# Where the shifted copies of the offset maps come from: nine copies within SBUF, or one write to memory and three shifted reads

## The chip, the cores and the metric

The kernel runs on one core of one Trainium2 chip. The metric is the device time of one execution in microseconds (us).

## The reference, cut to what matters

Input `x` is (4, 128, 32, 32) in float32: four images of 128 channels and 32 x 32 pixels. Two residual layers follow each other.

```python
x = x + L0(_gn(x), W, b)            # group norm, then a mixing of all pixels by squared cosine scores
x = x + L1(_gn(x), w1, b1, w2, b2, wd)

def L1(x, w1, b1, w2, b2, wd):
    offset = conv2d_same(conv2d_same(x, w1, b1), w2, b2)    # 3x3 convolutions, 128 and then 72 channels
    return relu(deform_conv(x, offset, wd, k=3, pad=1, dg=4))

def deform_conv(x, offset, wd, k=3, pad=1, dg=4):
    off = offset.reshape(B, dg, K, 2, H, W)                 # 4 groups x 9 taps x (dy, dx) = 72 maps
    ...
    val = gather(y0, x0) * (wy0 * wx0)[:, :, None] + ...    # bilinear sample at each tap's place
    return jnp.einsum('ogck,bgckhw->bohw', wr, val)
```

The 72 offset maps say, for each pixel, where each of the nine taps of each of the four groups samples the image.

## The kernel before

The four images (batches b = 0 to 3) are worked on one after the other, with the engines' programs written out by hand as loops over slots: a batch has 72 slots n = 9 t + k, for eight tiles t of four image rows. While batch b is sampled and convolved, the same slots hold the front of the next ones: the mixing layer (scores, squares, products) of batch b + 2, the preparation of b + 3, and the two plain convolutions and the offsets of batch b + 1 (`conv_front`, by the table `STEADY`; for batch 0 they lie in a lead-in, by the table `LEAD`). Every engine takes its instructions strictly in the written order.

The kernel samples by place in memory and not by tap: a sample that tap k needs at pixel p is computed at p plus the tap's shift, and the last convolution reads it back with that shift. So each tap's eight offset maps are wanted in a copy that is shifted by `shift(k)` = 32 (k // 3 - 1) + k % 3 - 1 elements. The path of the offsets of one batch:

- VectorE writes the 72 maps into `off_ring` (L1164): 72 partitions, a ring `HELIX` = 1090 elements long, of which `TURN` = 33 at each end repeat the other end. `off_ring` lies in the tile `sim`.
- GpSimd fills those ends (`wrap_offsets`, L453 and L454) and raises `off_wrapped`.
- `shift_taps` (L292) copies, for each tap, eight partitions x 1024 elements from `off_ring` to `off_ch` (in the tile `combo`), at the tap's shift. SyncE's queue issues taps 0 to 4 (`BY_SYNC` = 5) and ScalarE's queue issues taps 5 to 8, both in slot `shift` (57 in the lead-in, 56 in the others). Each raises `off_shifted`.
- SyncE then writes the unshifted maps to the memory tensor `off_scr` (L332), which only the general path after the main loops reads back, where some offset reaches too far.
- TensorE transposes `off_ch` in slots 59 to 61 (`turn_offsets`, L614), behind a wait for all nine copies. In batch 1 it waits there for `gx_sum_done` too, by which VectorE reports the bias sums (L1091) for batch 3. VectorE places the result in `pos` (`place_in_order`, L1293 and L1297), makes the tents of the next batch's first tile (L1317 to L1326) and the products (`weights`, L1342), and adds out the first quarter of this batch (L1349).

```python
def shift_taps(eng, taps):
    for k in taps:
        rows = slice(2 * G * k, 2 * G * (k + 1))
        eng.dma_start(off_ch[rows, :], off_ring[rows, TURN - shift(k):TURN - shift(k) + NPIX])\
            .then_inc(s["off_shifted"], 16)
...
pe.wait_ge(s["off_shifted"], SHIFTS * (b + 1))      # in turn_offsets, SHIFTS = 16 * K
```

What SyncE issues in order for a batch: `cross` for tiles 0 to 5 (L340, two copies within SBUF of `hwin`, each behind `own_ready`), `shift_offsets` of the next batch, `cross` 6, the store of the first quarter (L346, behind VectorE's L1349), `cross` 7, three more stores. TensorE's samples (L695) wait for `cross`. ScalarE, in the slots around its four issues, moves windows out of PSUM (L891), samples to `val` (L910) and turned weights to `wcell` (L897), and for batch 3 makes `g_p` (L843). The last convolution is L719, in three pieces of six in slots 60 to 62.

Of the kernel before, what the change touches and what calls it, by code (L numbers as in the profile page):

```python
# [27 lines left out]
F32 = mybir.dt.float32  # L28
# [9 lines left out]
def mix_deform_kernel(nc, x, W0, b0, w1, b1, w2, b2, wd, out):  # L38
    B, C, H, WID = x.shape
    NPIX = H * WID  # L40
    HALF = NPIX // 2
    G, K = 4, 9
    CG = C // G
    NOFF = 2 * G * K
# [8 lines left out]
    TURN = WID + 1  # L53
    HELIX = NPIX + 2 * TURN
# [19 lines left out]
    with ctx:  # L74
# [57 lines left out]
        off_ch = combo[:, :, :, :].rearrange("p e i c -> p (e i c)")[0:NOFF, 0:NPIX]  # L132
# [97 lines left out]
            "swap_ready own_ready crossed_even crossed_odd dist_done fold_done tent_done weights_done turned turn_free "  # L230
            "sampled val_free dconv_done orelu_done yout_done settled grid_ready out_first out_second").split()}
        out_sems = [s["out_first"], s["out_second"]]
        off_scr = nc.dram_tensor("off_scr", [B, NOFF, NPIX], F32, kind="Internal").ap()

        block = ctx.enter_context(nc.Block())

        def batch(ap, b):
# [5 lines left out]
        MIX = [4 + 3 * i for i in range(QT)]  # L243
        SPREAD, KEEP, STATS = 1, 2, 26
        LEAD = dict(mean=31, dev=31, var=33, norm=34, combine=(35, 46), high=(35, 46), conv=(40, 51), wrap=57,
                    shift=57, turn={59: (0, 1), 61: (2, 3)}, extremes=65)
        STEADY = dict(mean=23, dev=24, var=25, norm=28, combine=(29, 42), high=(30, 43), conv=(35, 48), wrap=54,
                      shift=56, turn={60: (0, 1), 61: (2, 3)}, extremes=66)
        PREP_FIRST = ("normalise", "square", "high", "norms", "low", "invert", "bias", "diagonal")
        PREP_SECOND = {18: ("normalise",), 21: ("square",), 22: ("high",), 23: ("norms", "low"), 24: ("invert",),  # L250
                       27: ("diagonal",), 33: ("bias",)}
# [19 lines left out]
        TURNED0, SAMPLED0, FREE0, VAL0, YOUT0, DCONV0, ORELU0 = 1, 3, 2, 1, 2, 1, 2  # L271
        RIMS = 2
        ZEROED = 5
        SHIFTS = 16 * K
        BY_SYNC = 5
        CONV_INPUTS = 4 + K
        W_ROWS = SCORE[2] + 1
        CELL_STEPS = 30
# [5 lines left out]
        def shift(k):  # L284

            return WID * (k // 3 - 1) + k % 3 - 1

        def shift_taps(eng, taps):

            for k in taps:  # L290
                rows = slice(2 * G * k, 2 * G * (k + 1))
                eng.dma_start(off_ch[rows, :], off_ring[rows, TURN - shift(k):TURN - shift(k) + NPIX])\  # L292
                    .then_inc(s["off_shifted"], 16)

        def settle(eng):

# [16 lines left out]
        @block.sync  # L313
        def _(sp):
            sp.dma_start(x_all[:, 0, :], x[0].rearrange("c h w -> c (h w)")).then_inc(s["x_first_in"], 16)
            sp.dma_start(w0_sb[:, :], W0).then_inc(s["mix_weights_in"], 16)
            sp.dma_start(b0_row[:, :], b0.partition_broadcast(P)).then_inc(s["mix_weights_in"], 16)
            sp.dma_start(b1_col[:, :], b1).then_inc(s["conv_weights_in"], 16)
            for k in range(K):
                sp.dma_start(b2_col[2 * G * k:2 * G * (k + 1), :], b2.rearrange("(g k a) o -> k g a o", g=G, k=K)[k])\  # L320
                    .then_inc(s["conv_weights_in"], 16)
            for dst, src in zip(w_raw + [wd_sb[:, :]], (w1, w2, wd)):
                sp.dma_start(dst, src.rearrange("c k o -> c (k o)")).then_inc(s["conv_weights_in"], 16)
            sp.dma_start(x_all[:, 1:B, :], x[1:B].rearrange("b c h w -> c b (h w)")).then_inc(s["x_rest_in"], 16)
            for half in range(2):
                sp.nop().then_inc(out_sems[half], 16)
            sp.nop().then_inc(s["g_stored"], 16)
            def shift_offsets(b):

                sp.wait_ge(s["off_wrapped"], 2 * b + 2)  # L330
                shift_taps(sp, range(BY_SYNC))
                sp.dma_start(off_scr[bass.ds(b, 1), :, :].rearrange("b n q -> n (b q)"),  # L332
                             off_ring[:, TURN:TURN + NPIX]).then_inc(s["off_saved"], 16)

            def cross(b, t):

                sp.wait_ge(s["own_ready"], ROWT * b + t + 1)
                for r in range(2):
                    here, there = (slice(CELLS * h, CELLS * (h + 1)) for h in (r, 1 - r))
                    sp.dma_start(hwin[there, t % 2, :, 1, :], hwin[here, t % 2, :, 0, :])\  # L340
                        .then_inc(s["crossed_odd" if t % 2 else "crossed_even"], 16)

            def store(b, m):
                q = QORDER[m]
                sp.wait_ge(s["yout_done"], 4 * b + m + 1 + YOUT0)
                sp.dma_start(out[bass.ds(b, 1), :, 2 * BLK * q:2 * BLK * (q + 1), :].rearrange("b c h w -> c (b h w)"),  # L346
                             yout[:, m % 2, :]).then_inc(out_sems[m % 2], 16)

            shift_offsets(0)
            for b in range(B):  # L350
                for t in range(ROWT - 2):
                    cross(b, t)
                if b + 1 < B:
                    shift_offsets(b + 1)
                cross(b, ROWT - 2)
                store(b, 0)
                cross(b, ROWT - 1)
                for m in range(1, 4):
                    store(b, m)
            for half in range(2):  # L360
                sp.wait_ge(out_sems[half], 16 * (2 * B + 1))
            sp.wait_ge(s["off_saved"], 16 * B)
            with sp.If(is_beyond(sp)):
                with sp.Fori(0, B) as b:
                    sp.wait_ge(s["g_offT"], b + 1)
                    sp.dma_start(off_raw, off_scr[bass.ds(b, 1), :, :].rearrange("b n q -> n (b q)"))\
                        .then_inc(s["g_off"], 16)
                    with sp.Fori(0, ROWT) as t:
                        sp.wait_ge(s["g_out"], ROWT * b + t + 1)
                        sp.dma_start(out[bass.ds(b, 1), :, bass.ds(BLK * t, BLK), :].rearrange("b c h w -> c (b h w)"),  # L370
                                     yout[:, 0, 0:P]).then_inc(s["g_stored"], 16)
                sp.wait_ge(s["g_stored"], 16 * (B * ROWT + 1))
# [450 lines left out]
        def _(act):  # L823
# [34 lines left out]
                        act.activation(own.rel[:, j, :], own.scores[:, j, :], ACT.Relu).then_inc(s["rel_done"], 1)  # L858

            def conv_front(b, n, at):  # L860
                if n == at["shift"]:
                    act.wait_ge(s["off_wrapped"], 2 * b + 2)
                    shift_taps(act, range(BY_SYNC, K))
                if n == at["var"]:
                    std(b)
                for which in range(2):
                    m = 2 * b + which
                    if 0 <= n - at["high"][which] < V:
                        v = n - at["high"][which]
                        act.wait_ge(s["combo_done"], V * m + v + 1)  # L870
                        act.activation(combo_p[:, 0, v], combo[:, v % 2], ACT.Copy).then_inc(s["combo_hi"], 1)  # L871
                    if n == at["conv"][which] + 3:
                        bias, width = ((b1_col, C), (b2_col, NOFF))[which]
                        act.wait_ge(s["m_done"], V * m + 2)
                        act.activation(m1[0:width], psA[0:width, 1, :], ACT.Identity, bias=bias[:, :])\
                            .then_inc(s["m1_done"], 1)
# [671 lines left out]
```

## Time and profile before

| | us |
|---|---|
| median of 3 runs | 515.77 (515.76 to 515.89) |
| the profiled execution, its own time | 515.51 |
| its span, first to last instruction | 513.8 |
| TensorE matmuls busy | 428.8 (83%) |
| VectorE busy | 344.2 (67%) |
| ScalarE busy | 224.7 (44%) |
| GpSimd busy | 140.7 (27%) |

The profiled execution's own time is 1.7 us longer than its span, for what lies around the instructions, and 0.26 us under the median. TensorE's mean granted clock is 0.947 of full speed. Busy shares are means over stages with different limits, so they don't tell what a single stage waits for.

### The profile page before, as it was taken

What the parts mean: (1) busy time and instruction counts of PE and PEld (TensorE: products, weight loads), DVE (VectorE), ACT (ScalarE), POOL (GpSimd) and SP (SyncE); (2) the same over time, 40 slices, a digit from 0 to 9 for tenths busy, and PEclk for the clock granted to TensorE, in tenths of its full rate; (3) what the DMA queues carried; (4) which work ended last, traced back from release to release, by engine and by line L of the source; (5) the groups of instructions that cost most, each with busy time, mean ns of one, the idle gap of its engine ahead of it and who ended that gap; (6) DMA issues with size and microseconds to landing.
All of it is one profiled execution on the core that took longest, in us unless ns stands there. A gap on an engine that the chain in (4) does not pass through costs nothing.

```text
span 513.8 us, 9711 instructions
## 1 busy us (share of the span) xinstructions
PE 428.8 (83%) x3881; PEld 304.9 (59%) x3881; DVE 344.2 (67%) x582; ACT 224.7 (44%) x404; POOL 140.7 (27%) x179
## 2 busy tenths in 40 slices
PE   2899799967998988779998987878798976888886
PEld 2666465734665656557665654657565654666665
DVE  4619996499988983954657992745979538199400
ACT  2046133224565453414655453314765333178640
POOL 3266441343872102102763101101210101031100
PEclk9999799997999989989999989879998987999999
DMA  3400000201111113011101112011210121023211
GB/s 122 169 1 1 1 1 1 46 1 21 22 22 22 22 22 65 6 40 31 33 15 27 22 22 56 23 33 41 43 24 20 25 64 33 20 52 64 42 33 33
DMA packets 22187, 17.23 MB, mean 34 GB/s; under 512 B 1981, under 2 KB 20669, under 8 KB 22141
## 3 DMA queue, kind: packets, MB, share of 16 engines
q1 hardware_dynamic: 21884, 16.07, 12.9%
q10 hardware_dynamic: 256, 0.52, 0.7%
q8 instruction: 32, 0.52, 0.4%
q14 instruction: 15, 0.11, 0.1%
HBM read 3.74 MB, written 3.28 MB: 14 GB/s over the span
## 4 chain that ended last, share of the span: by engine, by line
PE 58%; DVE 24%; ACT 7%; issue 5%; DMA 3%; ACTq 2%; SPq 1%; DVEq 0%
PE psB L719 13%; PE psB L506 12%; PE psA L586 8%; DVE wpix L1342 6%; PE psV L695 5%; PE psA L506 5%; PE psT L672 5%; ACT wcell L897 3%; DVE tent L1323 2%; PE psT L662 2%; DMA hwin<-hwin 2%; PE psA L562 2%; DVE tent L1317 2%; DVE combo L1135 2%; ACT val L910 2%
## 5 line engine op out<-in xcount | busy, mean ns | idle before, releaser
L897 ACT ACTIVATE wcell<-psT 128x512 f32<-128x512 f32 (+1 forms) x160 | 83.4, 552 | 82.3 <-PE psT L672 73.6
L1342 DVE TENSOR_TENSOR wpix<-tent 128x512 f32<-128x512 f32 (+1 forms) x160 | 107.1, 720 | 16.0 <-PE psT L672 15.0
L672 PE MATMUL psT<-ident,wpix 128*128 128x128 f32 x576 | 86.5, 283 | 14.5 <-ACT wcell L897 13.5
L672 PEld LDWEIGHTS psT<-ident,wpix 128*128 128x128 f32 x576 | 66.9, 144 | 38.8 <-issue 28.7
L447 POOL COPY strips<-hring 128x256 f32<-128x256 f32 x64 | 43.3, 702 | 155.8 <-PE psT L662 155.8
L424 POOL TENSOR_TENSOR sim<-rel 128x512 f32<-128x512 f32 x48 | 60.3, 1276 | 62.4 <-ACT rel L858 62.4
L719 PE MATMUL psB<-val,wd_sb 128*128 128x256 f32 x288 | 73.5, 412 | 3.6 <-issue 3.6
L719 PEld LDWEIGHTS psB<-val,wd_sb 128*128 128x128 f32 x288 | 57.7, 206 | 15.6 <-issue 7.2
L695 PE MATMUL psV<-wcell,hwin 64*32 64x144 f32 x2048 | 48.5, 300 | 13.3 <-DMA hwin<-hwin 13.3
L910 ACT ACTIVATE val<-psV 128x576 f32<-128x576 f32 x64 | 44.0, 688 | 34.2 <-PE psV L695 22.7
L506 PE MATMUL psB<-g_p 128*128 128x512 f32 x144 | 44.6, 448 | 6.7 <-DVE g_p L1075 6.7
L1349 DVE TENSOR_TENSOR yout<-orelu,x_all 128x256 f32<-128x256 f32 x16 | 6.8, 423 | 64.0 <-ACT orelu L915 64.0
L506 PE MATMUL psA<-combo_p,w_p 128*128 128x512 f32 (+1 forms) x144 | 42.5, 443 | 4.2 <-DVE combo_p L1139 4.2
L586 PE MATMUL psA<-sim,scratch 128*128 128x512 f32 x96 | 45.6, 598 | 0.1
L695 PEld LDWEIGHTS psV<-wcell,hwin 64*32 64x32 f32 x2048 | 28.5, 109 | 25.3 <-issue 22.6
L858 ACT ACTIVATE rel<-psB 128x512 f32<-128x512 f32 x48 | 28.3, 598 | 24.6 <-PE psB L506 22.1
L506 PE MATMUL psB<-combo_p,w_p 128*128 128x512 f32 (+1 forms) x144 | 37.6, 411 | 0.0
L506 PEld LDWEIGHTS psB<-g_p 128*128 128x128 f32 x144 | 27.9, 203 | 16.1 <-DVE g_p L1075 7.0
L662 PE MATMUL psT<-ident,strips 128*128 128x128 f32 x128 | 20.1, 280 | 17.5 <-ACT wcell L897 17.5
L506 PEld LDWEIGHTS psA<-combo_p,w_p 128*128 128x128 f32 (+1 forms) x144 | 25.0, 180 | 15.7 <-issue 7.5
L871 ACT ACTIVATE combo_p<-combo 128x544 fp32r<-128x544 f32 x32 | 20.7, 657 | 28.9 <-DVE combo L1135 28.9
L506 PEld LDWEIGHTS psB<-combo_p,w_p 128*128 128x128 f32 (+1 forms) x144 | 23.2, 166 | 11.2 <-issue 1.3
(166 smaller groups left out, 498.0 us busy)
## 6 DMA issues: line engine op xcount, KB each, us to landing
hwin<-hwin SPq DMA_DIRECT2D x64, 128.0 KB, 2.5
out<-yout SPq DMA_DIRECT2D x16, 128.0 KB, 1.8
x_all<-x SPq DMA_DIRECT2D x1, 1536.0 KB, 8.9
off_scr<-sim SPq DMA_DIRECT2D x4, 288.0 KB
combo<-sim SPq DMA_DIRECT2D x20, 32.0 KB
val<-w SPq DMA_DIRECT2D x1, 576.0 KB
wd_sb<-wd SPq DMA_DIRECT2D x1, 576.0 KB
x_all<-x SPq DMA_DIRECT2D x1, 512.0 KB, 3.5
```

The lines of the kernel that those rows point to most:

```text
L424: pool.tensor_tensor(own.sim[:, i % 2, j * HALF:(j + 1) * HALF], own.rel[:, j, :], own.rel[:, j, :], ALU.mult)\
L447: pool.tensor_copy(strips[:, :, odd, :].rearrange("p m (r c) -> p m r c", c=SUP), src)\
L506: last = pe.matmul(dst, left[l], right[r], start=start and i == 0, stop=stop and i == 2)
L586: last = pe.matmul(own.sums[:, j, :], own.gx[:, i, :], own.sim[:, i % 2, j * HALF:(j + 1) * HALF], start=i == 0, stop=i == QT - 1)
L662: last = pe.transpose(bank[:, v * C:(v + 1) * C], strip, ident[:, :])
L672: last = pe.transpose(bank[:, at:at + P], wpix[:, t % 2, k, 2 * h:2 * h + 2, :].rearrange("p g q -> p (g q)"), ident[:, :])
L695: last = pe.matmul(bank[g * CG:(g + 1) * CG, e, :, m, :], hwin[rows, t % 2, u // 2, (u + r) % 2, g * CG:(g + 1) * CG], w[:, :, :, BLK * u: ...
L719: last = pe.matmul(bank, wd_sb[:, k * C:(k + 1) * C], val[:, k, at:at + 2 * P], start=k == 0, stop=k == K - 1)
L858: act.activation(own.rel[:, j, :], own.scores[:, j, :], ACT.Relu).then_inc(s["rel_done"], 1)
L897: act.activation(wcell[:, t % 2, taps[0]:taps[-1] + 1, :, :].rearrange("q k h p -> q (k h p)"), bank[:, 0:len(taps) * G // 2 * P], ACT.Cop ...
L910: act.activation(dst, src, ACT.Copy).then_inc(s["val_free"], 1)
L1342: dve.tensor_tensor(w, ty, tx, ALU.mult).then_inc(s["weights_done"], 1)
```

## The change

`off_scr` is made `HELIX` wide. For each batch SyncE writes the whole ring, 72 rows of 1090 elements, to `off_scr`, waits for `off_saved`, and then issues three transfers from `off_scr` back to `off_ch`, one per row of taps: 24 rows of 1024 elements each. The source pattern steps by 8 * 1090 - 1 from one tap to the next, so that the tap's shift is in the step. ScalarE's four issues and the slot `shift` are gone; `off_shifted` now counts three transfers. The general path reads the middle of the wider rows.

```diff
-        off_scr = nc.dram_tensor("off_scr", [B, NOFF, NPIX], F32, kind="Internal").ap()
+        off_dram = nc.dram_tensor("off_scr", [B, NOFF, HELIX], F32, kind="Internal")
+        off_scr = off_dram.ap()
...
-        SHIFTS = 16 * K
-        BY_SYNC = 5
+        SHIFTS = 16 * 3
...
-        def shift_taps(eng, taps):
-
-            for k in taps:
-                rows = slice(2 * G * k, 2 * G * (k + 1))
-                eng.dma_start(off_ch[rows, :], off_ring[rows, TURN - shift(k):TURN - shift(k) + NPIX])\
-                    .then_inc(s["off_shifted"], 16)
+        def shifted(b, y):
+
+            at = (b * NOFF + 3 * y * 2 * G) * HELIX + TURN - shift(3 * y)
+            return bass.AP(off_dram, at, [[2 * G * HELIX - 1, 3], [HELIX, 2 * G], [1, NPIX]])
...
             def shift_offsets(b):
 
                 sp.wait_ge(s["off_wrapped"], 2 * b + 2)
-                shift_taps(sp, range(BY_SYNC))
-                sp.dma_start(off_scr[bass.ds(b, 1), :, :].rearrange("b n q -> n (b q)"),
-                             off_ring[:, TURN:TURN + NPIX]).then_inc(s["off_saved"], 16)
+                sp.dma_start(off_scr[b, :, :], off_ring).then_inc(s["off_saved"], 16)
+                sp.wait_ge(s["off_saved"], 16 * (b + 1))
+                for y in range(3):
+                    sp.dma_start(off_ch[3 * 2 * G * y:3 * 2 * G * (y + 1), :], shifted(b, y)).then_inc(s["off_shifted"], 16)
...
             def conv_front(b, n, at):
-                if n == at["shift"]:
-                    act.wait_ge(s["off_wrapped"], 2 * b + 2)
-                    shift_taps(act, range(BY_SYNC, K))
```

On SyncE's queue, for batch 1 (`combo` holds `off_ch`, `sim` holds `off_ring`), there stood before:

```order
L340 DMA hwin<-hwin 64x4x128 [waits own_ready]
L340 DMA hwin<-hwin 64x4x128
L292 DMA combo<-sim 8x1024 [waits off_wrapped]
L292 DMA combo<-sim 8x1024 x4
L332 DMA off_scr<-sim 72x1024
L340 DMA hwin<-hwin 64x4x128 [waits own_ready]
```

and now:

```order
L339 DMA hwin<-hwin 64x4x128 [waits own_ready]
L339 DMA hwin<-hwin 64x4x128
L329 DMA off_scr<-sim 72x1090 [waits off_wrapped]
L332 DMA combo<-off_scr 24x1x1024 [waits off_saved]
L332 DMA combo<-off_scr 24x1x1024 x2
L339 DMA hwin<-hwin 64x4x128 [waits own_ready]
```

Six issues without a wait among them have become one, a wait for that one's landing, and three. What follows in the queue stands behind that wait.

On ScalarE, in slots 55 to 58 of batch 1's front, there stood before:

```order
L838 ACTIVATE rel<-inv_all 128x1024 [waits g_done]
L891 ACTIVATE hwin<-psT 128x4x128 [waits turned]
L292 DMA combo<-sim 8x1024 [waits turn_free,off_wrapped]
L292 DMA combo<-sim 8x1024 x3
L910 ACTIVATE val<-psV 128x9x4x16 [waits sampled]
L897 ACTIVATE wcell<-psT 128x512 [waits turned]
L843 ACTIVATE g_p<-inv_all 128x1024 [waits simps_done,g_done]
```

and now:

```order
L837 ACTIVATE rel<-inv_all 128x1024 [waits g_done]
L887 ACTIVATE hwin<-psT 128x4x128 [waits turned]
L906 ACTIVATE val<-psV 128x9x4x16 [waits turn_free,sampled]
L893 ACTIVATE wcell<-psT 128x512 [waits turned]
L842 ACTIVATE g_p<-inv_all 128x1024 [waits simps_done,g_done]
```

The four issues are gone and nothing else has moved; TensorE's, VectorE's and GpSimd's instructions stand in the same order as before.

## Rows read from the trace of the kernel before

**Rows 1.** The page: the span, and the chain that ended last by engine.

```profile
span 513.8 us, 9711 instructions
...
PE 58%; DVE 24%; ACT 7%; issue 5%; DMA 3%; ACTq 2%; SPq 1%; DVEq 0%
```

**Rows 2.** The chain that ended last, 312 to 350 us: start, length, what.

```profile
315.76 0.72 ACTq L292
...
323.38 0.63 PE psA L614 x8
...
332.32 0.35 DVE yout L1349
...
334.15 2.64 DMA hwin<-hwin
```

**Rows 3.** Timeline, batch 2's offsets: start, length, what, [idle before <- releaser].

```profile
314.19 3.45 SPq L292 DMA_DIRECT2D combo<-sim  x5
...
315.06 2.91 ACTq L292 DMA_DIRECT2D combo<-sim  x4
...
319.32 0.41 PE L672 MATMUL psT<-ident,wpix 128*128 128x128 f32 x2 [3.33 <-ACT wcell L897]
...
320.46 2.93 PE L719 MATMUL psB<-val,wd_sb 128*128 128x256 f32 x6
...
323.18 0.45 PE L614 MATMUL psA<-ident,combo 72*128 72x72 f32 x2
...
323.85 1.51 PE L719 MATMUL psB<-val,wd_sb 128*128 128x256 f32 x6
...
329.05 0.72 PE L695 MATMUL psV<-wcell,hwin 64*32 64x144 f32 x32
```

**Rows 4.** Timeline, batch 1's offsets.

```profile
197.64 3.42 SPq L292 DMA_DIRECT2D combo<-sim  x5
...
204.33 0.41 PE L672 MATMUL psT<-ident,wpix 128*128 128x128 f32 x2 [0.52 <-ACT wcell L897]
...
207.84 0.34 PE L614 MATMUL psA<-ident,combo 72*128 72x72 f32 x2 [0.96 <-DVE scratch L1091]
```

**Rows 5.** Timeline, batch 0's offsets, in the lead-in.

```profile
92.23 3.45 SPq L292 DMA_DIRECT2D combo<-sim  x5
...
101.80 0.29 PE L614 MATMUL psA<-ident,combo 72*128 72x72 f32 x2
```

**Rows 6.** Timeline, batch 3's offsets.

```profile
409.13 3.47 SPq L292 DMA_DIRECT2D combo<-sim  x5
...
417.58 0.45 PE L614 MATMUL psA<-ident,combo 72*128 72x72 f32 x2
```

**Rows 7.** DMA packets in the stretches 90 to 102, 0 to 10 and 125 to 130 us.

```profile
DMA packets 228, 0.59 MB, mean 49 GB/s; under 512 B 84, under 2 KB 84, under 8 KB 228
...
DMA packets 685, 0.66 MB, mean 66 GB/s; under 512 B 301, under 2 KB 557, under 8 KB 685
...
DMA packets 544, 0.26 MB, mean 52 GB/s; under 512 B 32, under 2 KB 544, under 8 KB 544
```

**Rows 8.** By stretch: PE, PEld, DVE, ACT, POOL busy, PEclk, DMA share, GB/s.

```profile
16.00:18.00 2.00, 2.00 (x11) 2.00 (x10) 0.00 (x0) 0.00 (x0) 0.00 (x0) 1.00 1.02 420
93.00:97.00 4.00, 4.00 (x24) 2.96 (x23) 0.00 (x0) 1.33 (x2) 0.00 (x0) 1.00 0.37 59
97.00:99.30 2.30, 2.30 (x19) 2.21 (x19) 0.78 (x3) 0.81 (x2) 1.90 (x2) 1.00 0.54 153
```

**Rows 9.** The page, DMA issues: size, us to landing.

```profile
out<-yout SPq DMA_DIRECT2D x16, 128.0 KB, 1.8
...
x_all<-x SPq DMA_DIRECT2D x1, 512.0 KB, 3.5
```

**Rows 10.** TensorE alone by stretch: PE busy, PEclk, DMA share, GB/s.

```profile
218.00:219.00 1.00, 0.00 (x0) 1.00 0.38 131
...
222.00:223.00 1.00, 1.00 (x9) 0.50 0.00 0
```

More of the change, by code:

```diff
@@ L245, in mix_deform_kernel @@
         LEAD = dict(mean=31, dev=31, var=33, norm=34, combine=(35, 46), high=(35, 46), conv=(40, 51), wrap=57,
-                    shift=57, turn={59: (0, 1), 61: (2, 3)}, extremes=65)
+                    turn={59: (0, 1), 61: (2, 3)}, extremes=65)
         STEADY = dict(mean=23, dev=24, var=25, norm=28, combine=(29, 42), high=(30, 43), conv=(35, 48), wrap=54,
-                      shift=56, turn={60: (0, 1), 61: (2, 3)}, extremes=66)
+                      turn={60: (0, 1), 61: (2, 3)}, extremes=66)
         PREP_FIRST = ("normalise", "square", "high", "norms", "low", "invert", "bias", "diagonal")
@@ L365, in _ @@
                     sp.wait_ge(s["g_offT"], b + 1)
-                    sp.dma_start(off_raw, off_scr[bass.ds(b, 1), :, :].rearrange("b n q -> n (b q)"))\
+                    sp.dma_start(off_raw, off_scr[bass.ds(b, 1), :, TURN:TURN + NPIX].rearrange("b n q -> n (b q)"))\
                         .then_inc(s["g_off"], 16)
```

## The prediction

> **What bounds the kernel now.** I read the page first: 513.8 us of span, and a chain of 58% TensorE and 24% VectorE, with only 2% in ScalarE's queue and 1% in SyncE's [rows 1]. So no engine's total decides, and I looked for the change's place in the chain by time. There, at batch 2's offsets, the chain runs through ScalarE's issues, then TensorE's turn (L614), VectorE's tents, the add of the first quarter, its store, and the last `hwin` crossing (2.64 us of DMA), behind which TensorE's sample waits [rows 2]. From the turn on, VectorE's order leaves no slack, so the time at which the turn begins is what counts. The timelines show what the turn waits for now. I count from t0, at which SyncE issues the first shift, because `off_wrapped` doesn't depend on the change. The first turn begins at t0 + 9.57 in batch 0 [rows 5], + 10.20 in batch 1 [rows 4], + 8.99 in batch 2 [rows 3] and + 8.45 in batch 3 [rows 6]. The copies have landed well before: no gap ahead of a turn names them. In batch 0 TensorE is simply busy until then. In batch 1 it waits 0.96 us for VectorE's L1091, which stands behind ScalarE's `g_p`, and before that 0.52 us for a `wcell`. In batches 2 and 3 ScalarE sits in its four issues (2.91 us) and TensorE idles 3.33 us for `wcell` [rows 3]. So the change does two things to each turn: it lets the engines be ready sooner, and it makes the data come later.
>
> **What is taken away.** ScalarE's four issues cost 2.91 us a batch. Batch 0: TensorE has no gap there, so nothing is won. Batch 1: both gaps close, 0.96 + 0.52 = 1.5 us, and the turn could begin at t0 + 8.7. Batches 2 and 3: the gap of 3.33 us closes, and the six L719 ahead of the turn, 2.93 us long where the next six take 1.51 [rows 3], run at full clock, 1.4 us less; TensorE is ready at about t0 + 4.3 and + 3.7. If the data came in time, that would be a gain of over 10 us. It decides nothing unless the data come in time. SyncE's five shifts and the old write (3.45 us and an issue more) go too; they are replaced next.
>
> **What is added: a write, a wait, three reads.** How many of the 16 DMA engines a transfer uses can be counted. In 90 to 102 us nine shifts of 8 rows and one write of 72 rows are all that moves: 228 packets, of which 84 are small [rows 7]. The other 144 are the 9 x 8 + 72 rows; 84 = 9 x 8 + 12, one small packet for each DMA engine that takes part, 8 for a shift, 12 for the write. The two crossings of 256 pieces from 64 partitions have 544 = 512 + 32: 16 engines each. In 0 to 10 us, after 16 each for `x`, `W0` and `b0` and 128 + 16 for `b1`, 301 leaves 109 [rows 7]: one of another queue and nine times 12 for the `b2` loads, 8 for data and 4 for engines. Those loads have 8 partitions on one side and 4 groups of 2 on the other. All of this fits one reading: the number is the largest, up to 16, that divides the outermost counts of both sides. A read of the change has 24 rows on one side and 3 groups of 8 rows on the other, so it would use 3 DMA engines, and each would carry 8 rows of 4 KB. The same three would carry all three reads, 24 rows each, if the lowest ones are always taken, which no row shows. The Trainium skill states just this rule in "DMA: Bandwidth & Descriptors", section "Why a DMA increments its semaphore by 16 and not by 1", and adds that the lowest-numbered engines are used; the trace agrees in its counts. It speaks against this change.
>
> The time of a 4 KB row on one DMA engine: loads from memory in 16 to 18 us move 420 GB/s at a share of 1.02, so 16 x 2.0 x 1.02 us for 205 rows, 0.16 us. The stretch 97.0 to 99.3, mostly the write to memory, gives 16 x 2.3 x 0.54 us for 352 KB or 86 rows, 0.23 us. The stretch 93 to 97, mostly shifts from unaligned places within SBUF, gives 16 x 4.0 x 0.37 us for 58 rows, 0.41 us [rows 8]. Fixed parts: a store of 128 KB lands in 1.8 us, 1.5 without its two rows' worth per engine (0.32); the load of 512 KB lands in 3.5 us, 2.2 without its 8 rows (1.28) [rows 9].
>
> Write: it is nearest to the store and to the 0.23 us rows: 1.5 + 6 rows x 0.23 x 1.06 for the longer rows = 3.0 us. Bounds: 1.5 + 6 x 0.16 = 2.5, and 1.5 + 6 x 0.41 x 1.06 = 4.1. Reads: issues follow each other by some 0.69 us (3.45 for five [rows 3]), while three engines need 8 x 0.16 = 1.28 us for one, so the engines and not the queue set the end. They are loads from memory into SBUF, nearest to `x`: 2.2 + 24 x 0.16 = 6.05 us after the first issue. Bounds: 1.5 + 3.84 = 5.3, and 2.2 + 24 x 0.41 = 12.0. With 0.05 us for SyncE to go on, the last read lands at t0 + **9.1**, between + 7.9 and + 16.2.
>
> A fixed part from a page: the Trainium skill, "DMA: Bandwidth & Descriptors", section "Anatomy of one DMA", puts some 2.0 us on a DMA (it says so of the GpSimd path), most of it the receipt from the target. With two such in a row this part would be an estimated 4.0 us in place of 1.5 + 2.2, and the sum about 1 us higher; the trace's store, 1.8 us in all, disagrees for writes to memory.
>
> Turn by turn, with landing at + 9.1. Batch 0: before + 9.57, no change. Batch 1: 9.1 - 10.2 = -1.1. Batch 2: 9.1 - 8.99 = +0.1, and batch 3: 9.1 - 8.45 = +0.65. Beside these stands TensorE's clock. It now idles from about + 4.3 to + 9.1 ahead of the turn, 4.8 us. In 218 to 219 us TensorE idles too, and in 222 to 223 the granted clock is 0.50, 1.2 GHz of 2.4 [rows 10]. So I take the six L719 between the first and the second turn at 2.93 us and not 1.51 [rows 3], and VectorE's second `pos` stands behind them: +1.4 us each in batches 2 and 3. Sum: 0 - 1.1 + 1.5 + 2.05 = **+2.5 us** against 515.5 of the profiled execution, or 518.3 against the median, which lies 0.26 higher.
>
> **At no cost.** Crossing 6 is behind the wait and three issues in SyncE's queue, some 1 us later than now, and behind the reads on three DMA engines: it lands near t0 + 10, and its sample is at t0 + 14.9 in batch 2 (329.05 [rows 3]). If that cover went, each microsecond would delay the sample and not yet the chain, which runs on VectorE there. The wider rows cost 6% of the write, counted. The count of waits on TensorE is the same. GpSimd and VectorE wait for `off_saved` and `off_shifted` only in the next batch. What is late next, once the turn is right, is the tents and products of VectorE as now.
>
> **Rivals.** (a) *The reads are spread.* If only the 24 rows of the destination counted, as 72 rows gave 12 engines, each engine would have 2 rows of each read. The third, issued 1.4 us after the first, lands at 3.05 + 1.4 + 2.2 + 0.3 = + 7.0. Batch 1 gains its 1.5 us, batch 2 2.0, batch 3 1.45, and the shorter idle leaves the clock out of it: -4.9 us, 510.9. It decides from a landing before about + 7.5 with the slow clock between the turns, + 8.9 without. For it: 24 rows are what the destination has. Against: the `b2` loads, whose 8 rows met 4 groups and gave 4. Three different triples of engines for the three reads would land them at 3.05 + 1.4 + 2.2 + 1.28 = + 7.9, and give -0.3 with the slow clock, -3.1 without. By the Trainium skill, "DMA: Bandwidth & Descriptors", section "Rules for kernel authors", small transfers should be joined to large ones, since below 64 KB overhead is most of the time; nine of 32 KB would become three of 96 KB, and this rival is what that rule would give.
> (b) *The data are just not late.* With both fixed parts at 1.5 and the fast rows, landing at + 7.9 gives 0 - 1.5 + 0.3 + 0.85 = -0.35 us: 515.4; and up to + 8.6 it stays within 0.2%. If the clock stayed full in addition, it would be 2.8 us less, 512.6.
> (c) *The rows are slow.* The sources start at odd places in memory, as those of the slow shifts did in SBUF. At 0.23 us a row the landing is + 10.8, and the four turns are late by 1.2, 0.6, 3.2 and 3.7: +8.7, 524.5. At 0.41 us and the slow write it would be + 16.2 and some +30 us, 546. For memory to SBUF I hold the rows of `x` to be the better measure.
> (d) *The change doesn't do what it says*, and each transfer is cut into pieces as small as before. Issued by SyncE alone, this would show as more packets, and comes out like (c).
>
> **How the numbers follow.** About 0.2% or 1.03 us is what a measurement of this kernel can tell from no change. Forecast (landing + 8.6 to + 10.3, +1.1 to +7 us): 0.55. Slow rows, (c) and (d): 0.11. Not late, (b): 0.15. Spread over more engines, (a): 0.19. That makes slower 0.66, same 0.15, faster 0.19. The range reaches from 512.5, the lower case of (b), to 524.5, the 0.23 us rows; it leaves out most of (a) and the end of (c), about 0.2.
>
> **What would show it.** Right: a window around one batch's offsets with 144 rows and 12 + 3 x 3 small packets, 165 in all; the last read landing near t0 + 9; TensorE's turn with a gap that names the DMA, some 0.6 us in batch 1 and 4 to 5 us in batches 2 and 3; ScalarE's `val` right behind its `hwin`; L719 between the turns at 2.9 us. Wrong: 12 + 3 x 12 small packets, a DMA share well above 3 / 16 in the reads, turns earlier than t0 + 8 in batches 2 and 3. The size is wrong if the reads go on for much more than 4 us.

## The result, and the profile after

The change makes the kernel slower: 521.84 us (median of 4 runs, 519.32 to 523.3) against 515.83 (515.76 to 516.09), a ratio of 1.011 with a 95% interval of 1.0071 to 1.015. The forecast of slower was right and the range of 512.5 to 524.5 us held it; the size was not, +6.0 us where +2.5 stood. The profiled execution took 521.55 us, its span 519.8, 6.0 more than before.

The page of the kernel after, for [rows 1], with the costliest lines of its chain and what is new among the DMA issues:

```profile
span 519.8 us, 9687 instructions
...
PE 58%; DVE 19%; DMA 8%; ACT 7%; issue 5%; SPq 2%; POOL 0%; DVEq 0%; ACTq 0%
PE psB L505 13%; PE psB L718 12%; PE psA L585 8%; PE psV L694 5%; PE psT L671 5%; PE psA L505 5%; DVE wpix L1338 4%; DMA combo<-off_scr 3%; ACT wcell L893 3%; PE psT L661 2%; DVE combo L1131 2%; ACT val L906 2%; DMA off_scr<-sim 2%; DMA hwin<-hwin 2%; PE psA L561 1%
...
off_scr<-sim SPq DMA_DIRECT2D x4, 306.6 KB
combo<-off_scr SPq DMA_DIRECT2D x12, 96.0 KB
```

DMA has gone from 3% of the chain to 8%, and both halves of the round trip stand in it by name; ScalarE's queue is down from 2% to 0%. No engine works longer: TensorE is busy for 429.1 us and was for 428.8.

Batch 2 in the timeline of the kernel after, against [rows 3] (lines have moved by one or four):

```profile
315.81 0.34 SPq L329 DMA_DIRECT2D off_scr<-sim  x1
...
318.01 0.41 PE L671 MATMUL psT<-ident,wpix 128*128 128x128 f32 x2 [0.39 <-ACT wcell L893]
...
319.00 1.56 PE L718 MATMUL psB<-val,wd_sb 128*128 128x256 f32 x6
...
319.24 2.33 SPq L332 DMA_DIRECT2D combo<-off_scr  x3
321.62 1.35 SPq L339 DMA_DIRECT2D hwin<-hwin  x2
326.31 0.50 PE L613 MATMUL psA<-ident,combo 72*128 72x72 f32 x2 [5.75 <-DMA combo<-off_scr]
...
327.33 2.86 PE L718 MATMUL psB<-val,wd_sb 128*128 128x256 f32 x6
...
337.30 0.41 DVE L1345 TENSOR_TENSOR yout<-orelu,x_all 128x256 f32<-128x256 f32 x1
```

ScalarE's relief is there: the gap of 3.33 us ahead of L671 is down to 0.39, and the six matmuls before the turn take 1.56 us in place of 2.93. TensorE then stands still for 5.75 us until the reads land, and the six matmuls between the turns take 2.86 us where they took 1.51. The first quarter is added (L1345) 21.5 us after t0; it was 18.1.

The other turns of the kernel after, for [rows 4] and [rows 6]:

```profile
197.47 0.32 SPq L329 DMA_DIRECT2D off_scr<-sim  x1
...
200.56 2.32 SPq L332 DMA_DIRECT2D combo<-off_scr  x3
...
208.34 0.32 PE L613 MATMUL psA<-ident,combo 72*128 72x72 f32 x2 [0.76 <-DMA combo<-off_scr]
```

```profile
412.15 0.34 SPq L329 DMA_DIRECT2D off_scr<-sim  x1
...
416.05 2.34 SPq L332 DMA_DIRECT2D combo<-off_scr  x3
...
423.15 0.50 PE L613 MATMUL psA<-ident,combo 72*128 72x72 f32 x2 [6.25 <-DMA combo<-off_scr]
```

DMA packets of the kernel after, 92 to 105 us, batch 0's offsets alone, for [rows 7]: the GB/s of 40 slices of 0.325 us, then the counts.

```profile
GB/s 0 0 0 0 0 80 215 188 188 201 81 13 0 0 0 0 0 13 13 25 50 76 88 76 76 76 76 76 88 88 76 13 0 0 0 0 0 0 0 0
DMA packets 165, 0.61 MB, mean 47 GB/s; under 512 B 21, under 2 KB 21, under 8 KB 165
```

165 packets, 21 of them small, are 144 rows, 12 engines of the write and 3 of each of three reads. The write runs at some 200 GB/s; the reads stay at some 76 for 3.6 us, which is 25 GB/s on each of three engines or 0.16 us a row. In the trace's packets the first row of the reads starts 1.6 us after the first read's issue, the first row on each of the three engines takes 0.49 to 0.70 us and every other 0.16, and the turn begins 0.52 us after the last row's end; the rows lie within 4.50 us.

What the steps were, in us after t0:

| batch | write landed | first read's issue to turn | first turn, before -> after | between the turns, before -> after | tents begin, before -> after |
|---|---|---|---|---|---|
| 0 | 3.1 | 6.6 | 9.57 -> 9.73 | 3.66 -> 3.68 | 11.39 -> 11.57 |
| 1 | 3.1 | 7.8 | 10.20 -> 10.87 | 2.04 -> 1.87 | 14.08 -> 14.56 |
| 2 | 3.4 | 7.1 | 8.99 -> 10.50 | 2.01 -> 3.67 | 12.82 -> 16.25 |
| 3 | 3.9 | 7.1 | 8.45 -> 11.00 | 2.58 -> 3.67 | 12.86 -> 16.76 |

The tents are 0.2 + 0.5 + 3.4 + 3.9 = 8.0 us later in all, and the end 6.0. These two don't belong together as they stand. From one t0 to the next the two profiled executions compare so, with the time at which TensorE's granted clock was 0.50, from the trace's clock record:

| stretch | us, before -> after | of these at 0.50 |
|---|---|---|
| start to batch 0's t0 (the same code) | 92.23 -> 93.07 | 10.2 -> 10.2 |
| batch 0's t0 to batch 1's | 105.41 -> 104.40 | 10.2 -> 6.8 |
| batch 1's to batch 2's | 116.55 -> 118.34 | 6.8 -> 17.1 |
| batch 2's to batch 3's | 94.94 -> 96.34 | 17.1 -> 13.7 |
| batch 3's to the end | 104.67 -> 107.65 | 10.2 -> 10.2 |

So 0.8 of the 6.0 us lie ahead of anything that was changed, 1.8 in a batch whose tents are only 0.5 later, and batches 2 and 3 keep 1.4 and 3.0 us of their 3.4 and 3.9.

### The profile page after: what moved, and what is told of

It reads as the page before. It is cut to its first block, busy times and chain, and to the rows that moved or that the text cites. A ratio compares the mean times of both kernels' runs of the same rounds, so it can differ in the third digit from the quotient of the medians.

```text
span 519.8 us, 9687 instructions
## 1 busy us (share of the span) xinstructions
PE 429.1 (83%) x3881; PEld 306.4 (59%) x3881; DVE 344.5 (66%) x582; ACT 225.1 (43%) x404; POOL 141.6 (27%) x179
## 4 chain that ended last, share of the span: by engine, by line
PE 58%; DVE 19%; DMA 8%; ACT 7%; issue 5%; SPq 2%; POOL 0%; DVEq 0%; ACTq 0%
PE psB L505 13%; PE psB L718 12%; PE psA L585 8%; PE psV L694 5%; PE psT L671 5%; PE psA L505 5%; DVE wpix L1338 4%; DMA combo<-off_scr 3%; ACT wcell L893 3%; PE psT L661 2%; DVE combo L1131 2%; ACT val L906 2%; DMA off_scr<-sim 2%; DMA hwin<-hwin 2%; PE psA L561 1%
## 5 line engine op out<-in xcount | busy, mean ns | idle before, releaser
L1338 DVE TENSOR_TENSOR wpix<-tent 128x512 f32<-128x512 f32 (+1 forms) x160 | 107.8, 724 | 16.3 <-PE psT L671 15.2
L671 PE MATMUL psT<-ident,wpix 128*128 128x128 f32 x576 | 86.4, 283 | 8.3 <-ACT wcell L893 7.2
L671 PEld LDWEIGHTS psT<-ident,wpix 128*128 128x128 f32 x576 | 67.1, 145 | 32.4 <-issue 23.1
L718 PEld LDWEIGHTS psB<-val,wd_sb 128*128 128x128 f32 x288 | 58.3, 208 | 15.5 <-issue 6.9
L694 PE MATMUL psV<-wcell,hwin 64*32 64x144 f32 x2048 | 48.1, 298 | 12.8 <-DMA hwin<-hwin 12.7
L1345 DVE TENSOR_TENSOR yout<-orelu,x_all 128x256 f32<-128x256 f32 x16 | 6.8, 423 | 63.4 <-ACT orelu L911 63.4
```

Source lines behind the costliest of these rows:

```text
L671: last = pe.transpose(bank[:, at:at + P], wpix[:, t % 2, k, 2 * h:2 * h + 2, :].rearrange("p g q -> p (g q)"), ident[:, :])
L694: last = pe.matmul(bank[g * CG:(g + 1) * CG, e, :, m, :], hwin[rows, t % 2, u // 2, (u + r) % 2, g * CG:(g + 1) * CG], w[:, :, :, BLK * u: ...
L718: last = pe.matmul(bank, wd_sb[:, k * C:(k + 1) * C], val[:, k, at:at + 2 * P], start=k == 0, stop=k == K - 1)
L1338: dve.tensor_tensor(w, ty, tx, ALU.mult).then_inc(s["weights_done"], 1)
```

## The experiments

Times are medians, and ratios (with their 95% intervals) are to the kernel before on the same chip; that one took 515.2 to 515.7 there. The runs beside each other lie on several chips, so two kernels of different sections are compared by their ratios. Edits are to the change, unless said otherwise.

**Even rows.** The step between taps without its shift, so one pattern of 24 rows.

```diff
-            return bass.AP(off_dram, at, [[2 * G * HELIX - 1, 3], [HELIX, 2 * G], [1, NPIX]])
+            return bass.AP(off_dram, at, [[HELIX, 3 * 2 * G], [1, NPIX]])
```

> The change, but the three reads take their 24 rows at an even step, so the shift by one element from tap to tap within a row of taps is left out; bytes, rows and number of transfers stay. Theory 'three engines' (a read with 3 groups on one side runs on 3 DMA engines): each read now runs on 12 engines, 12 + 3 x 12 = 48 small packets per batch in place of 21; the last read lands about 3.1 + 1.4 + 2.2 + 0.3 = t0 + 7.0 to + 7.8, the turns of batches 2 and 3 begin there in place of + 10.5 and + 11.0, batch 1's at about + 8.7; 511 to 513 us. Rival 'round trip' (a write and a read one after the other are slow whatever the engines): landing stays at + 9.7 to + 11, 520 to 523 us.

508.77 us, ratio 0.985 (0.9792 to 0.9907). Its packets in 92 to 105 us, and its batch 2:

```profile
DMA packets 192, 0.61 MB, mean 47 GB/s; under 512 B 48, under 2 KB 48, under 8 KB 192
```

```profile
316.70 1.15 SPq L332 DMA_DIRECT2D combo<-off_scr  x3
...
320.31 0.34 PE L613 MATMUL psA<-ident,combo 72*128 72x72 f32 x2 [1.95 <-DMA combo<-off_scr]
```

48 small packets are 12 + 3 x 12. From the first read's issue to the turn it takes 3.6 us in batches 2 and 3, in place of 7.1, with the same bytes, rows and number of transfers. The turns of batches 2 and 3 begin at + 6.7 and + 7.5. One more thing changes with the step: the three issues take 1.15 us and not 2.33, which accounts for 0.8 us of the 3.5, since the last read is issued that much sooner. The rival of a dear round trip falls: with 12 engines the write and the reads, one after the other, bring turns at + 6.7 and + 7.5 where the kernel before had + 9.0 and + 8.5. ScalarE is relieved here as in the change, so its part is in these times too. The time is below the 511 to 513 us that were expected; its four runs spread from 504.97 to 512.24.

**Reads twice.** Each read issued a second time, into a spare tile.

```diff
-                for y in range(3):
-                    sp.dma_start(off_ch[3 * 2 * G * y:3 * 2 * G * (y + 1), :], shifted(b, y)).then_inc(s["off_shifted"], 16)
+                for y in range(3):
+                    for dst in (off_twice, off_ch):
+                        sp.dma_start(dst[3 * 2 * G * y:3 * 2 * G * (y + 1), :], shifted(b, y)).then_inc(s["off_shifted"], 16)
```

> The change, with every read issued twice, the first time into a tile that nobody uses; the computation is whole. Theory 'three engines': 48 rows on three engines in place of 24, at 0.16 us each, so each read phase grows by 3.8 us: 10.4 to 10.9 us from the first read's issue to the turn in place of 6.6 to 7.8, 30 small packets per batch, and 14 to 16 us more in all than the change. Rival (a fixed price per transfer or per round trip): three more issues of 0.75 us on the queue, 2.3 us per batch at most.

540.88 us, one run: 16.3 more than the change on the same chip (524.56), where 14 to 16 were expected. Batch 0:

```profile
96.04 0.81 SPq L334 DMA_DIRECT2D off_twice<-off_scr  x1
...
106.66 0.43 PE L615 MATMUL psA<-ident,combo 72*128 72x72 f32 x2 [4.01 <-DMA combo<-off_scr]
```

10.6 us in place of 6.6: 24 rows more on each engine for 4.0 us, 0.167 us each. With the count of packets, rate and number of engines are both shown.

**Write in three.** Three writes of 24 rows on semaphores of their own, then each read behind its own.

```diff
-                sp.dma_start(off_scr[b, :, :], off_ring).then_inc(s["off_saved"], 16)
-                sp.wait_ge(s["off_saved"], 16 * (b + 1))
+                saved = [s["off_saved"], s["off_saved1"], s["off_saved2"]]
+                for y in range(3):
+                    rows = slice(3 * 2 * G * y, 3 * 2 * G * (y + 1))
+                    sp.dma_start(off_scr[b, rows, :], off_ring[rows, :]).then_inc(saved[y], 16)
                 for y in range(3):
+                    sp.wait_ge(saved[y], 16 * (b + 1))
```

> The change, with the write cut into three of 24 rows, and each read behind its own write only. Theory 'three engines': the reads queue on the same three engines as before, but the first begins when 24 rows have landed, about t0 + 2.1 in place of + 3.1 to + 3.9, so the last lands 1 to 1.8 us sooner, + 8.7 to + 9.3: 4 to 6 us less than the change, 516 to 518 us. Rival 'round trip is paid per transfer': three writes in a row land no sooner than one, 521 to 523 us.

519.16 us, ratio 1.0075 (1.0047 to 1.0103): clear of the change's second run (1.018, below) and not of its first (1.011). In the trace half of it came: in batches 0 and 1 the first read is issued at + 2.0 and + 1.9, and batch 1's turn is at + 9.3. In batches 2 and 3 it is issued only at + 3.4 and + 3.6, and the turns stay at + 10.5 and + 10.9. What stands beside the late writes there is in the last experiment.

**Crossing first.** Crossing 6 between the write and the wait.

```diff
                 sp.dma_start(off_scr[b, :, :], off_ring).then_inc(s["off_saved"], 16)
+                if between is not None:
+                    cross(*between)
                 sp.wait_ge(s["off_saved"], 16 * (b + 1))
```

> The change, with crossing 6 of hwin issued between the write and the wait for it, and not behind the reads. In the change the reads took 6.6 us from first issue to turn in batch 0, where no crossing follows, and 7.8, 7.1 and 7.1 in the others. If the crossing's packets on the three engines slow them: 6.6 us in all four, and 1 to 2 us less in all, 519.5 to 521 us. If not (the rival): no change in the reads, 521 to 523 us.

521.12 us, ratio 1.0132 (1.0081 to 1.0183): in the time it can't be told from the change. In the trace it can. From the first read's issue to the turn it now takes 6.8, 6.8, 6.8 and 6.6 us, where it took 6.6, 7.8, 7.1 and 7.1, and the turns of batches 1 to 3 are 0.4 to 0.5 earlier than in the change's profile. Part of what the reads gain is lost ahead of them: in batch 1 the crossing's two issues run until + 3.7, and the first read is issued there and not at + 3.1. So the crossing's packets, which share the three engines, look dear, but batch 0 has no crossing and varied too. Two more kernels were run on one chip to settle it.

**Crossing last**, and the crossing first once more.

```diff
                 if b + 1 < B:
                     shift_offsets(b + 1)
+                    sp.wait_ge(s["off_shifted"], SHIFTS * (b + 2))
                 cross(b, ROWT - 2)
```

> The change, with SyncE waiting for all three reads to land before it issues crossing 6, so that nothing of the crossing can lie beside a read. So far the time from the first read's issue to the turn was 7.1 to 7.8 us with the crossing behind the reads in batches 1 to 3, 6.6 to 6.8 with the crossing first, but also 6.6 to 7.2 in batch 0, where there is none. If the crossing slows the reads: 6.6 to 6.9 in batches 1 to 3, at least 0.3 less than in the change beside it. If the difference is from execution to execution (the rival): the same as batch 0 in the same run, 7.0 or more in some. The crossing lands near t0 + 13.5, before its sample at + 16 to + 18, so it costs nothing itself; 520 to 524 us.

> The kernel with crossing 6 first, a second time and on the same chip as the one with the crossing last. If the crossing slows the reads: again 6.6 to 6.8 us in batches 1 to 3. If not, anything from 6.6 to 7.8, as in the change.

Last: 519.62 us, ratio 1.0085 (1.0058 to 1.0112), 6.8, 6.7, 6.7 and 6.7 us. First again: 522.45 us (two runs), ratio 1.014 (1.0109 to 1.017), 6.8, 6.8, 6.7 and 6.8 us; its first reads are issued at + 3.7, + 3.9 and + 4.1, and the turns are at + 10.5, + 10.6 and + 10.8, so of the earlier turns only batch 1's came again. Batch 2 with the crossing last:

```profile
316.29 2.34 SPq L332 DMA_DIRECT2D combo<-off_scr  x3
...
322.95 1.35 SPq L339 DMA_DIRECT2D hwin<-hwin  x2
```

Nine batches with the crossing out of the way lie at 6.6 to 6.8 us, and eleven with it behind the reads (the change twice, the write in three, and without the relief, as far as the DMA ended the wait) at 7.1 to 7.8. The means are 6.7 and 7.25. In the packets, 420 to 460 of the crossing's 512 pieces, about 27 on each engine at 0.04 us each, lie before the reads' last row, and the rows take 5.0 to 5.7 us where they take 4.6 to 4.8 without. So the crossing goes with 0.3 to 1.1 us more, 0.5 on the mean. It isn't all that varies: in batch 0, which has no crossing, four kernels have 6.6 to 6.8 us, but the change's second run has 7.2, with four rows of 0.36 to 0.71 us in the later reads and no other packet beside them, and in that one profile batches 1 to 3 are no slower (7.2 to 7.3). Without the relief batch 0 has 7.0, with the four spare copies near it.

Held back, the crossing costs nothing: its sample comes much later. With the crossing last the four turns are 1.7 us earlier in all than in either profile of the change. The time agrees in sign, but its ratio of 1.0085 is clear only of the change's second run (1.018) and not of its first (1.011).

**Without the relief.** ScalarE issues four copies again in its old slot, into a spare tile.

```diff
+                if n == (57 if b == 0 else 56):
+                    act.wait_ge(s["off_wrapped"], 2 * b + 2)
+                    for k in range(5, K):
+                        rows = slice(2 * G * k, 2 * G * (k + 1))
+                        act.dma_start(off_idle[rows, :], off_ring[rows, TURN - shift(k):TURN - shift(k) + NPIX])\
+                            .then_inc(s["off_shifted"], 16)
```

> The change, with ScalarE's four issues put back in their old slot as copies into a tile that nobody uses (the computation is whole). Theory: while the data land at + 10 to + 11, what ScalarE was relieved of is worth nothing: the turns of batches 2 and 3 begin when the reads land, as in the change, and TensorE's idle time ahead of them is split in two, 3.3 us early and about 1.5 late, so the six matmuls between the turns may run at full clock again. 521 to 525 us where the change has 524.6 on this chip. Rival (the relief carried part of the change's time): 527 or more.

521.41 us, ratio 1.0127 (1.0087 to 1.0168), no slower than the change (1.011 and 1.018). Batch 2:

```profile
321.91 0.62 PE L672 MATMUL psT<-ident,wpix 128*128 128x128 f32 x2 [3.07 <-ACT wcell L900]
...
327.73 0.34 PE L614 MATMUL psA<-ident,combo 72*128 72x72 f32 x2 [1.71 <-DMA combo<-off_scr]
...
328.29 2.37 PE L719 MATMUL psB<-val,wd_sb 128*128 128x256 f32 x6
```

The turns come when the reads land, at + 10.7 and + 10.9; tents in batch 2 begin at + 15.5 where the change has + 16.3. The idle time is in two pieces, as expected (3.07 and 1.71 us); the matmuls between the turns don't get back to 1.5 us (2.37), which was not.

**Nine by SyncE**, from the kernel before: `BY_SYNC = K`, and ScalarE issues none.

```diff
-        BY_SYNC = 5
+        BY_SYNC = K
...
-                if n == at["shift"]:
-                    act.wait_ge(s["off_wrapped"], 2 * b + 2)
-                    shift_taps(act, range(BY_SYNC, K))
```

> The kernel before, with all nine shifts within SBUF issued by SyncE and none by ScalarE. No memory in between. Theory: the relief of ScalarE is worth what the gaps say once the data are in time. Nine issues of 0.69 us, the last one starts at t0 + 5.5 and lands at + 7.3 to + 7.7; batch 1 gains 1.5 us, batch 2 about 1.4, batch 3 about 1.0: 511.5 to 512.5 us. Rival (the relief is eaten, by the clock that falls in the idle time or by VectorE): 515.2 to 516 us.

513.86 us, ratio 0.9989 (0.9962 to 1.0016): no difference that can be told, where 511.5 to 512.5 us was expected. The profiled execution is the fastest of its ten (510.69). In it batch 1's tents begin 2.0 us earlier, at + 12.0. Batch 2:

```profile
311.61 6.57 SPq L292 DMA_DIRECT2D combo<-sim  x9
...
320.01 0.35 PE L614 MATMUL psA<-ident,combo 72*128 72x72 f32 x2 [3.65 <-DMA combo<-sim]
...
320.58 2.15 PE L719 MATMUL psB<-val,wd_sb 128*128 128x256 f32 x6
```

The turn is 0.6 us earlier than before, but it stands behind 3.65 us of idle time, the six matmuls take 2.15 us and the tents begin at + 13.0, as before (+ 12.8). Here relief without timely data is seen alone, in batches 2 and 3.

**Seven and two, six and three, and the slot alone.** From the kernel before: ScalarE's shifts stand two slots later in batches 1 to 3, behind its urgent copies, and SyncE takes 7, 6 or 5 of the nine.

```diff
-        BY_SYNC = 5
+        BY_SYNC = 6
...
-                      shift=56, turn={60: (0, 1), 61: (2, 3)}, extremes=66)
+                      shift=58, turn={60: (0, 1), 61: (2, 3)}, extremes=66)
```

> The kernel before, with seven shifts issued by SyncE and two by ScalarE, and ScalarE's two moved from slot 56 to slot 58 in batches 1 to 3, behind its urgent copies. No memory in between. Theory: the last shift starts at t0 + 4.1 and lands at about + 6; in batches 2 and 3 TensorE is ready at + 4.8, idles little over 1 us, and goes on at full clock: turns near + 6, the six matmuls between the turns in 1.5 us, 2.5 to 3 us less in each of these batches and 1.5 to 2 in batch 1; 508 to 510 us where the kernel before has 515.2. Rival (what is won at the turn is lost behind it): 513 to 516.

> As the kernel with seven and two, but six by SyncE and three by ScalarE in slot 58. The last of SyncE's starts at t0 + 3.5, the last of ScalarE's at + 3.6 in batches 2 and 3 and + 6 in batch 1: turns near + 5.5 in batches 2 and 3, + 8.4 in batch 1; 507.5 to 510 us.

> The kernel before with one edit: ScalarE's four shifts stand in slot 58 in batches 1 to 3 and not in slot 56; five and four as before. It tells the place of the issues from their split. Theory: in batches 2 and 3 ScalarE is through with its urgent copies at t0 + 2.1, its last shift starts at + 4.3 and lands near + 6.2, turns at + 6.3 to + 6.7; in batch 1 it starts at + 4.5 and its last lands near + 8.5, turn at + 8.5 to + 8.8; 507.5 to 510 us, within 1 us of six and three. Rival (the gain of six and three came from the shorter ScalarE list): 512 or more.

Seven and two: 509.95 us, ratio 0.9883 (0.9846 to 0.9921). Six and three: **507.55 us, ratio 0.9856 (0.9835 to 0.9876)**, the fastest kernel of the study that computes the whole. Both were expected so, at 508 to 510 and 507.5 to 510. The slot alone: 511.66 us, ratio 0.9923 (0.9898 to 0.9948), where 507.5 to 510 was expected. So the place alone gains, and the split adds to it; by the medians each is about half of the gain, which the intervals leave open. The profile of the slot alone is of its fastest run, 507.23 us, where the other five took 510.6 to 512.3, so it doesn't show what six and three has over it. Six and three in batch 2:

```profile
312.48 4.55 SPq L292 DMA_DIRECT2D combo<-sim  x6
...
313.37 0.69 ACT L910 ACTIVATE val<-psV 128x576 f32<-128x576 f32 x1
...
314.60 1.29 ACTq L292 DMA_DIRECT2D combo<-sim  x2
...
319.01 0.35 PE L614 MATMUL psA<-ident,combo 72*128 72x72 f32 x2 [1.77 <-DMA combo<-sim]
...
319.57 1.51 PE L719 MATMUL psB<-val,wd_sb 128*128 128x256 f32 x6
```

Its turns begin at + 8.4, + 6.5 and + 6.3 in batches 1 to 3. With the slot alone batch 1's is at + 9.5, after a wait of 0.93 us that names the shifts; the others are at + 6.4.

**The change again**, on the chip of the runs beside it.

> The change itself, on the chip of the runs beside it, for what differs from execution to execution. If the distance to the kernel before is the change's and not the chip's, it is 5 to 8 us again, and the reads again take 6.6 us in batch 0 and 7 to 8 in the others, and the write 3.1 us where no packet of the instruction queue shares its stretch, 3.4 to 3.9 where one does.

524.56 us (523.79 to 525.21), ratio 1.018 (1.0163 to 1.0198): 8.9 us over the kernel before there. The reads took 7.2 us in batch 0, where 6.6 to 6.8 stands in four other kernels, and 7.3, 7.2 and 7.2 in the others. The write landed after 3.1 us in batches 0 to 2 and 4.0 in batch 3. DMA by queue in this run, 413.4 to 417.5 us:

```profile
DMA packets 86, 0.34 MB, mean 83 GB/s; under 512 B 12, under 2 KB 12, under 8 KB 84
...
q8 instruction: 1, 0.02, 2.2%
q14 instruction: 1, 0.01, 0.5%
```

In the stretches of the other three writes there are 84 packets and none of these queues. The same holds over all runs with this write: with nothing from the instruction queues (q8, q14) in its stretch it landed after 3.1 us, also in batch 2 with even rows and with the reads twice, and with a q8 packet of 0.02 MB beside it after 3.4 to 4.3. In the write in three both late writes had one. The size fits only in part. A q8 packet is 16 KB, an estimated 0.65 us at the reads' 25 GB/s on one engine, but the last written row ends only 0.2 us later in the change's batch 2 and 0.65 later in batch 3, and the landing 0.3 and 0.8 later. And in the write in three SyncE's issue of the third write lasts 1.83 and 1.93 us in batches 2 and 3 and 0.37 in the others, so the issuing itself was held up beside these packets. No run took the packets away, so which of the two counts, and whether either is the cause, stays open.

## Why the prediction was right in its way and wrong in its size

- **Three engines.** Right: 12 + 3 x 3 small packets, 0.16 us a row, and even rows and doubled reads say the same. That all three reads took the same three engines follows from their 76 GB/s together. Rival (a) falls with it, and (c) and (d) fall as causes, though the turns came where (c) had put the landing, + 10.8, for other reasons. The Trainium skill says that the number of engines is the largest, up to 16, that divides the outermost counts of both sides, in "DMA: Bandwidth & Descriptors", section "Why a DMA increments its semaphore by 16 and not by 1"; the trace agrees with it for the shapes counted here: 24 rows against 3 groups give 3, 24 against 24 give 12.
- **The write**, 3.0 us: right in batches 0 and 1 (3.1), 0.4 and 0.9 short in batches 2 and 3, where instruction packets stood beside it: 1.3 us in all.
- **The reads**, 6.05 us, are the term that was most short: 7.8, 7.1 and 7.1 us in batches 1 to 3, 3.8 us in all. Of this 0.6 to 0.7 a batch is there with nothing beside the reads (6.6 to 6.8; the change's second profile, batch 0, has 7.2, which stays open). The packets say where: 1.6 us to the first row and 0.5 from the last row's end to the turn are the 2.2 us of the fixed part, and 24 rows take 4.5 to 4.8 us and not 3.84; the first row on each engine is slow, 0.5 to 0.7 us in batch 0. The later row's 0.16 us was right (4.0 us for 24 more).
- **Crossing 6 at no cost.** This is where a sentence of the prediction fails outright. I had asked what the reads do to the crossing, not what the crossing does to the reads: with it behind them they took 0.3 to 1.1 us more in batches 1 to 3. The turns came at + 10.9, + 10.5 and + 11.0 in place of + 9.1, and in the prediction's own working each such microsecond counts once a batch.
- **Turn by turn.** Batch 1 was to gain 1.1 and lost 0.5 to 0.7; batches 2 and 3 were to lose 0.1 and 0.65 at the turn and lost 1.5 and 2.55. The sum over these three is 5.1 us more than forecast: 3.8 of the reads and 1.3 of the write. All three landings lie outside the + 8.6 to + 10.3 that the forecast was tied to.
- **The clock.** Right in its direction and near in size: 3.67 between the turns where 2.01 and 2.58 stood, so +1.7 and +1.1 for +1.4 each. That the charge would be partly paid back was not foreseen. Before, TensorE idled 4.64 us ahead of batch 2's last crossing and its sample ran 1.21 us; after, it idled 3.29 there and the sample ran 0.72. From there to the next t0 the kernel after needs 70.8 us and the one before 72.3. That is one part of what lies between the tents' 8.0 and the end's 6.0; the rest is in stretches that differ without the change's doing (the table of stretches above), in which the clock was granted otherwise. By the prediction's own sum, which counts what each turn is late and what the slower clock adds, the turns as they came give an estimated + 7.6 us. So the range held the time in part by luck: the landings were worse than its upper end allowed, and 2 us or more came back elsewhere.
- **The relief.** Right in kind: a gain if the data come in time, and nothing otherwise. Nine by SyncE and the copies into a spare tile show the nothing. The "over 10 us" was not reached by any kernel: six and three, which keeps three of ScalarE's issues but behind its urgent copies, shows 8.2 us, and even rows, with the full relief and its data at + 6.7 and + 7.5, 6.5.

For the clock, the idle time ahead of the first turn of batches 2 and 3, and from the first turn to the second, over the runs:

| kernel | idle ahead | between the turns |
|---|---|---|
| slot moved | 1.69, 1.60 | 1.90, 1.91 |
| six and three | 1.77, 1.57 | 1.90, 1.91 |
| even rows | 1.95, 2.72 | 1.90, 1.90 |
| seven and two | 2.29, 2.07 | 2.52, 1.90 |
| nine by SyncE | 3.65, 3.18 | 2.51, 2.89 |
| without the relief | 3.07 + 1.71, 3.07 + 1.89 | 2.72, 2.82 |
| the change | 5.75, 6.25 | 3.67, 3.67 |

The granted clock of the kernel after in its longest case, TensorE alone (length of the stretch, then busy us and matmuls, granted clock, DMA share, GB/s), for [rows 10]:

```profile
324.00:325.00 1.00, 0.00 (x0) 1.00 0.48 102
325.00:326.00 1.00, 0.00 (x0) 0.62 0.18 67
326.00:327.00 1.00, 0.69 (x6) 0.50 0.11 32
328.00:329.00 1.00, 1.00 (x4) 0.50 0.00 0
```

TensorE waits for the reads from 320.56 on. The grant stands at 1.00, 2.4 GHz, until 325.24, so it falls within the idle time and not at the turn; from there to 332.07 it is 0.50, 1.2 GHz, and four matmuls of the second run fill a microsecond. The table shows the same step: where TensorE had one idle time of 1.6 to 2.7 us, the piece between the turns takes 1.9 us in seven cases of eight, after 3.2 and 3.7 us it takes 2.9 and 2.5, and after 5.8 and 6.3 us 3.7. The last idle time alone doesn't tell: without the relief it was 1.7 and 1.9 us, but another of 3.07 us had ended 4 us before it began, and the piece took 2.7 and 2.8.

## What to carry to other kernels

Before joining small transfers into large ones, count the engines that each will use, by its small packets in a trace: nine copies on 8 engines each beat three reads on the same 3 with the same bytes, because the step that joins three taps in one pattern takes the engines away. Nine reads of 8 rows from memory, which would keep the shifts and should use 8 engines each by the counts above, were not run. Ask of every queue entry near a critical transfer both what it waits for and what it slows. Where an engine must issue transfers, try them behind its urgent work before handing them to another engine: here the place alone gained (ratio 0.9923), and handing all nine over alone did not (0.9989).

## What the runs showed that I had not expected

- The price of an issue on SyncE goes with the pattern: 0.7 to 0.8 us for a read with the shift in its step, on 3 engines, 0.38 for an even one on 12 (1.15 for three), 0.32 to 0.36 for the write. The number of engines doesn't settle it, since a shift within SBUF on 8 engines takes 0.69 and a crossing on 16 takes 0.67.
- The write landed in 3.1 us within 0.1, except beside packets of the instruction queues.
- Batch 0's t0, up to which all kernels are the same code, lay at 90.8 to 91.2 us in seven profiles and at 92.2 to 93.1 in seven others, and the kernel with the crossing first has one of each (90.80 and 92.86). So a microsecond or two between single executions says nothing here; the kernel before itself went from 513.5 to 516.5 us on one chip. What sets it was not looked into.
